# Attention with the high and low halves of v in one matmul of 66 columns, and x loaded already turned

## What is computed

```
q, k, v = (x @ W + b for W, b in ...)          # split in 12 heads of 32
scores  = q @ k.T / sqrt(32) + beta * adj
scores  = where(adj > 0, scores, -9e15)
out     = softmax(scores) @ v
```

## Time and profile before

| | |
|---|---|
| median of 3 runs | 2648.01 us (2646.37 to 2648.55) |
| the profiled execution | 2648.33 us |
| its span, first to last instruction | 2646.3 us |
| mean granted TensorE clock | 0.984 of full speed |
| busy: PE, PEld, DVE, ACT, POOL | 95%, 71%, 80%, 78%, 84% |
| HBM read, written | 35.92 MB, 12.58 MB |

### The profile page before, as it was taken

The page is one execution under the profiler, slowest core; times in us unless marked ns, Lnnn a source line. Parts: engine busy times, 40 slices in busy tenths (PEclk is TensorE's granted clock), DMA queues, the critical chain, the costliest instruction groups (busy, mean ns, idle before and its releaser), DMA issues.

```text
span 2646.3 us, 91774 instructions
## 1 busy us (share of the span) xinstructions
PE 2513.5 (95%) x33856; PEld 1892.1 (71%) x33856; DVE 2112.3 (80%) x8230; ACT 2075.7 (78%) x5844; POOL 2230.9 (84%) x3340
## 2 busy tenths in 40 slices
PE   5799999999999999999999999999999999999985
PEld 4667677777777777777777777777777777777753
DVE  6687787877778888888888888888888888888874
ACT  6667877778778888888888788788788888888765
POOL 5488888888888898898888888888888888888874
PEclk9899999999999999999999999999999999999997
DMA  6834545545445555545545555554545555554533
GB/s 176 176 68 83 97 85 97 96 83 97 89 87 97 95 90 97 97 89 95 97 89 100 93 90 98 96 91 93 96 95 92 93 99 88 96 97 88 94 55 71
DMA packets 846822, 251.63 MB, mean 95 GB/s; under 512 B 805552, under 2 KB 845616, under 8 KB 846384
## 3 DMA queue, kind: packets, MB, share of 16 engines
q1 hardware_dynamic: 837920, 230.83, 50.3%
q10 hardware_dynamic: 8464, 14.94, 1.9%
HBM read 35.92 MB, written 12.58 MB: 18 GB/s over the span
## 4 chain that ended last, share of the span: by engine, by line
POOL 35%; PE 23%; DVE 16%; ACT 13%; issue 7%; DMA 5%; SPq 1%; DVEq 0%; ACTq 0%; POOLq 0%
POOL region L750 6%; ACT region L870 5%; DMA region<-region 4%; POOL region L739 4%; DVE region L1138 4%; PE bank L966 3%; PE bank L957 3%; PE bank L968 3%; PE bank L967 3%; PE bank L959 3%; PE bank L958 3%; ACT region L876 3%; POOL ab L766 3%; POOL region L790 2%; DVE small L1144 2%
## 5 line engine op out<-in xcount | busy, mean ns | idle before, releaser
L957 PE MATMUL bank<-region,w_hi 128*128 128x128 f16 x3960 | 690.4, 220 | 35.6 <-DVE w_lo L1075 14.0
L959 PE MATMUL bank<-region,w_lo 128*128 128x128 f16 x3960 | 690.0, 220 | 0.0
L958 PE MATMUL bank<-region,w_hi 128*128 128x128 f16 x3960 | 690.0, 220 | 0.0
L966 PE MATMUL bank<-w_hi,region 128*128 128x384 f16 x1815 | 595.5, 328 | 10.4 <-DMA region<-region 9.2
L967 PE MATMUL bank<-w_lo,region 128*128 128x384 f16 x1815 | 594.3, 327 | 0.0
L968 PE MATMUL bank<-w_hi,region 128*128 128x384 f16 x1815 | 594.2, 327 | 0.0
L750 POOL TENSOR_TENSOR region<-region 128x512 f16<-128x512 f32 x330 | 382.9, 1161 | 117.7 <-ACT region L876 116.6
L870 ACT ACTIVATE region<-region,small 128x128 f32<-128x128 f32 x1320 | 419.2, 389 | 53.6 <-DVE small L1144 44.1
L957 PEld LDWEIGHTS bank<-region,w_hi 128*128 128x128 f16 x3960 | 389.4, 98 | 60.8 <-issue 36.2
L958 PEld LDWEIGHTS bank<-region,w_hi 128*128 128x128 f16 x3960 | 389.8, 98 | 14.8 <-issue 9.9
L959 PEld LDWEIGHTS bank<-region,w_lo 128*128 128x128 f16 x3960 | 389.9, 98 | 0.0
(11 more groups left out here) (246 smaller groups left out, 8238.0 us busy)
## 6 DMA issues: line engine op xcount, KB each, us to landing
region<-region SPq DMA_TRANSPOSE x825, 3.0
last_unit<-w_dram ACTq DMA_DIRECT2D x19, 576.0 KB, 6.2
x<-x_dram SPq DMA_DIRECT2D x55, 192.0 KB, 2.3
out_dram<-region SPq DMA_DIRECT2D x55, 192.0 KB, 2.2
adj<-adj_dram SPq DMA_DIRECT2D x55, 64.0 KB, 2.2
mask<-adj_t_dram SPq DMA_DIRECT2D x55, 64.0 KB, 2.4
rows<-rows_dram ACTq DMA_DIRECT2D x5, 576.0 KB, 4.4
last_unit<-last_unit SPq DMA_TRANSPOSE x135, 3.1
```

Of the source, the lines that this page charges most:

```text
L957: pe.matmul(dst, lhsT=w_hi[:, w, k, cols], rhs=t_hi[u][:, k, :], start=(k == 0), stop=False)
L958: pe.matmul(dst, lhsT=w_hi[:, w, k, cols], rhs=t_lo[u][:, k, :], start=False, stop=False)
L959: last = pe.matmul(dst, lhsT=w_lo[:, w, k, cols], rhs=t_hi[u][:, k, :], start=False, stop=(k == DT - 1))
L966: pe.matmul(dst, lhsT=t_hi[u][:, k, :], rhs=w_hi[:, w, k, :], start=(k == 0), stop=False)
```

## The change

Five things change.

1. In attend, v_hi and v_lo of a head stand side by side as one moving operand of 66 columns. Two matmuls a head instead of three: p_hi x (v_hi, v_lo) to 66 columns, then p_lo x v_hi added to the first 33. ScalarE copies the first 33 of each head out, and a new VectorE step adds the other 33 to the copy. This add now frees the bank.
2. The host passes x also turned. It is loaded first, into the place of z; ScalarE and GpSimd write the halves straight to t_hi and t_lo, and the first DMA transpose of a unit falls away. x and the adjacency are loaded after ScalarE's cast. The load into the slot waits for the norm (886) of unit i - 7, not for line 1256.
3. denominator moves from GpSimd to VectorE: two one-column operations at the end of delta_di, a reciprocal in the place of the power.
4. minus_adjacency moves from GpSimd to ScalarE.
5. All wish times of the plan and the tables SHIFTED and ARRIVES are new (PERIOD 22.1046 becomes 22.0705), so all engines' lists change order; the weight counters follow the list's own order (nth).

```diff
-    "attend": lambda s: {...}.get(s, (SCALAR, "attend", s))
+    "attend": lambda s: {...}.get(s, (VECTOR, "attend", s))
+        x_t = [a[:, 0:D].rearrange("p (t n) -> p t n", n=N) for a in z_at]
+        v_both = [a.bitcast(F16).rearrange("p (a h c) -> p a h c", a=2, c=HS) for a in v_at]
+        def two_parts(made):
+            return made[:, 0:2 * GO].rearrange("p (h a c) -> p h a c", a=2, c=HS)
...
 SyncE
-            def load(i, k):
+            def load_turned(i, k):
...
-                    sp.wait_ge(*mixed_out.at(i - UNITS, "added", 3))
+                    sp.wait_ge(*scalar_done.at(i - UNITS, "normed", 3))
+                sp.dma_start(x_t[i % UNITS], x_t_d[i]).then_inc(loaded.of(i), 16)
+            def load(i, k):
+                sp.wait_ge(*cast.at(i, "x", 0))
                 sp.dma_start(x[i % UNITS], x_d[i]).then_inc(loaded.of(i), 16)
                 sp.dma_start(adj[i % UNITS], adj_d[i]).then_inc(loaded.of(i), 16)
...
 GpSimd
+                if k == 0:
+                    pool.tensor_tensor(t_lo[u], x_t[u], t_hi[u], ALU.subtract).then_inc(low_made.of(i), 1)
+                    return
...
-            def minus_adjacency(i, k):
-                pool.wait_ge(*mixed_out.at(i, "delta_gcn", 1))
-                pool.tensor_scalar(minus_adj[u], adj[u], -1.0, None, ALU.mult).then_inc(gpsimd_done.of(i), 1)
-            def denominator(i, layer):
-                pool.wait_ge(*mixed_out.at(i, "delta_di", layer))
-                pool.tensor_scalar(col(u, DENOM), col(u, ZSUM), 1e-10, col(u, DSUM), ALU.mult, ALU.add).then_inc(gpsimd_done.of(i), 1)
-                pool.wait_ge(*gpsimd_done.at(i, "sum", layer))
-                pool.tensor_tensor(col(u, INVERSE), col(u, DENOM), constant(MINUS_ONE), ALU.pow).then_inc(gpsimd_done.of(i), 1)
...
 ScalarE
-                act.wait_ge(w_lo_made, n - STAGES + 1)
+                act.wait_ge(w_lo_made, nth(VECTOR, WEIGHT_ORDER[n - STAGES]))
...
-                    act.wait_ge(*loaded.at(i, "in"))
-                    src = x
+                    act.wait_ge(*loaded.at(i, "turned"))
+                    act.activation(t_hi[i % UNITS], x_t[i % UNITS], ACT.Copy).then_inc(cast.of(i), 1)
+                    return
...
-                act.activation(z_at[u][:, t * GO:(t + 1) * GO], bank("attend", s, i)[:, 0:GO], ACT.Copy).then_inc(scalar_done.of(i), 1)
+                act.activation(o_un[u][:, t * HG:(t + 1) * HG, :], two_parts(bank("attend", s, i))[:, :, 0, :], ACT.Copy).then_inc(scalar_done.of(i), 1)
...
+            def minus_adjacency(i, k):
+                act.wait_ge(*mixed_out.at(i, "delta_gcn", 1))
+                act.activation(minus_adj[u], adj[u], ACT.Copy, scale=-1.0).then_inc(scalar_done.of(i), 1)
...
 TensorE
-                        pe.wait_ge(*scalar_done.at(j, "o", n))
+                        pe.wait_ge(*numbers.at(j, "heads", n))
...
-                pe.wait_ge(*landed.at(i, "x", TURN_OF[w]))
+                if TURN_OF[w] == 0:
+                    pe.wait_ge(*low_made.at(i, "x", 0))
+                else:
+                    pe.wait_ge(*landed.at(i, "x", TURN_OF[w]))
...
-                    dst = bank("attend", s, i)[:, g * HS:(g + 1) * HS]
+                    dst = two_parts(bank("attend", s, i))[:, g, :, :]
-                    pe.matmul(dst, lhsT=pt_hi[u][:, g, :], rhs=v_hi[u][:, h, :], start=True, stop=False)
-                    pe.matmul(dst, lhsT=pt_hi[u][:, g, :], rhs=v_lo[u][:, h, :], start=False, stop=False)
-                    last = pe.matmul(dst, lhsT=pt_lo[u][:, g, :], rhs=v_hi[u][:, h, :], start=False, stop=True)
+                    pe.matmul(dst, lhsT=pt_hi[u][:, g, :], rhs=v_both[u][:, :, h, :], start=True, stop=False)
+                    last = pe.matmul(dst[:, 0, :], lhsT=pt_lo[u][:, g, :], rhs=v_hi[u][:, h, :], start=False, stop=True)
...
 VectorE
-                    dve.wait_ge(*gpsimd_done.at(i, "minus"))
+                    dve.wait_ge(*scalar_done.at(i, "minus"))
+            def attend(i, s):
+                u, t = i % UNITS, s % DT
+                heads = o_un[u][:, t * HG:(t + 1) * HG, :]
+                dve.wait_ge(*scalar_done.at(i, "o", s))
+                dve.tensor_tensor(heads, two_parts(bank("attend", s, i))[:, :, 1, :], heads, ALU.add).then_inc(numbers.of(i), 1)
...
-                                         op1=ALU.add, accum_out=col(u, DSUM)).then_inc(mixed_out.of(i), 1)
+                                         op1=ALU.add, accum_out=col(u, DSUM)).then_inc(numbers.of(i), 1)
+                dve.wait_ge(*numbers.at(i, "row sum", layer))
+                dve.tensor_scalar(col(u, DENOM), col(u, ZSUM), 1e-10, col(u, DSUM), ALU.mult, ALU.add).then_inc(numbers.of(i), 1)
+                dve.wait_ge(*numbers.at(i, "denominator", layer))
+                dve.reciprocal(col(u, INVERSE), col(u, DENOM)).then_inc(mixed_out.of(i), 1)
...
 host
+        "x_t_dram": _np.ascontiguousarray(a["x"].reshape(B, N, DT, 128).transpose(0, 3, 2, 1)),
```

More of the change, by code:

```diff
@@ new lines @@
+    (POOL, "turn", 1): (-615.369, 0.869, 1.111, ((SCALAR, "turn", 1),), ()),
+    (VECTOR, "delta_gcn", 1): (-610.860, 0.199, 0.407, ((SCALAR, "u_gcn", 1),), ()),
+    (VECTOR, "project", 7): (-605.018, 0.463, 0.741, ((SCALAR, "project", 7),), ()),
+    (SCALAR, "attend", 4): (-585.092, 0.170, 0.300, ((PE, "attend", 4),), ()),
+    (POOL, "bias", 8): (-585.084, 0.955, 1.090, ((SCALAR, "project", 8),), ()),
+    (POOL, "inner", 2): (-578.725, 0.780, 0.900, ((SCALAR, "inner_spread", 2),), ()),
+    (SCALAR, "norm", 2): (-560.881, 0.598, 0.740, ((POOL, "residual", 2),), ()),
@@ new lines @@
+    (SCALAR, "norm", 3): (-328.787, 0.597, 0.740, ((POOL, "residual", 3),), ()),
+    (SCALAR, "project", 6): (-328.735, 0.370, 0.570, ((PE, "project", 6),), ()),
+    (PE, "project", 17): (-321.463, 1.466, 1.660, ((SYNC, "turn", 5),), ()),
+    (SYNC, "turn", 2): (-314.258, 1.240, 3.600, ((VECTOR, "turn", 2),), ()),
+    (VECTOR, "u_di", 1): (-311.228, 0.364, 0.632, ((PE, "u_di", 1),), ()),
+    (VECTOR, "delta_low", 1): (-311.002, 0.480, 0.460, ((SCALAR, "delta", 1),), ()),
+    (VECTOR, "add_bias", 11): (-309.625, 0.460, 0.560, ((PE, "project", 11), (POOL, "low", 9)), ()),
@@ new lines @@
+    (SCALAR, "delta", 1): (-186.860, 0.190, 0.310, ((VECTOR, "delta_di", 1),), ()),
+    (VECTOR, "turn", 4): (-183.196, 0.442, 0.718, ((SCALAR, "turn", 4),), ()),
+    (POOL, "inner", 3): (-170.708, 0.780, 0.900, ((SCALAR, "inner_spread", 3),), ()),
+    (SCALAR, "norm", 0): (-170.159, 0.599, 0.740, ((POOL, "residual", 0),), ()),
+    (PE, "scores", 0): (-166.086, 0.360, 0.610, ((VECTOR, "project", 2), (POOL, "low", 0), (POOL, "low", 1)), ()),
+    (PE, "project", 1): (-165.576, 1.513, 1.710, ((POOL, "turn", 0),), ()),
@@ new lines @@
+    (SCALAR, "project", 8): (-76.615, 0.370, 0.570, ((PE, "project", 8),), ()),
+    (VECTOR, "attend", 1): (-76.478, 0.200, 0.320, ((SCALAR, "attend", 1),), ()),
+    (POOL, "low", 9): (-73.290, 0.880, 1.120, ((SCALAR, "project", 9),), ()),
+    (VECTOR, "u_di", 0): (-72.133, 0.385, 0.656, ((PE, "u_di", 0),), ()),
+    (PE, "u_di", 1): (-70.812, 0.512, 0.720, ((SYNC, "turn", 4),), ()),
+    (VECTOR, "residual", 1): (-70.774, 0.480, 0.620, ((VECTOR, "gain", 1),), ()),
+    (SCALAR, "attend", 5): (-70.263, 0.170, 0.300, ((PE, "attend", 5),), ()),
@@ new lines @@
+    (POOL, "scores", 1): (177.943, 1.150, 1.420, ((SCALAR, "scores", 1),), ()),
+    (POOL, "bias_x", 0): (193.093, 0.961, 1.245, ((SYNC, "load", 0),), ()),
+    (POOL, "bias", 5): (254.100, 0.955, 1.090, ((SCALAR, "project", 5),), ()),
+    (VECTOR, "add_bias", 1): (257.477, 0.460, 0.720, ((PE, "project", 1),), ((SYNC, "store", 0),)),
+    (SCALAR, "minus_adj", 0): (442.166, 0.190, 0.300, ((VECTOR, "delta_gcn", 1),), ()),
+    (SCALAR, "turn", 5): (453.393, 0.413, 0.600, ((SCALAR, "norm", 2),), ()),
@@ L600, in graph_layers @@
         scalar_done = signal("scalar_done", SCALAR, {"attend": ("o",), "u_gcn": ("e_gcn",),
[L601 removed]
+                                                     "u_di": ("e_di",), "norm": ("normed",), "minus_adj": ("minus",), "delta": ("high delta",),
                                                      "spread": ("minus mean", "spread"),
@@ L621, in graph_layers @@
         gpsimd_done = signal("gpsimd_done", POOL, lambda name, k: {
-            "turn_delta": ("triangles",), "sides": ("upper", "lower"), "minus_adj": ("minus",),
-            "sums": ("sum", "row scale"),
+            "turn_delta": ("triangles",), "sides": ("upper", "lower"),
             "inner": ("inner root",) if k < 2 else ("variance", "inner root"),
@@ L663, in low_of, with nth @@
             return v_lo[u][:, :, 0:HD]
+        def nth(engine, w):
+            return 1 + [k for name, k, _ in sequence(engine) if name == "weight"].index(w)
         def load_weight(eng, n):
@@ L814, in _ @@
             for name, k, i in sequence(POOL):
```

(2 more changed lines are left out.)

417 lines of the change are left out of this document (194 added, 223 removed), and 60 rows, old and new, of the table SHIFTED.

## The result

The changed kernel takes 2656.3 us (median of 5 runs, 2652.22 to 2658.13) beside 2648.0 us (5 runs, 2642.6 to 2648.55) before: a ratio of 1.0033, 95% interval 1.0019 to 1.0046. It is 0.3% slower; the forecast was 2616.5 us, faster, with a range up to 2642. The profiled execution took 2656.3 us, of which 2653.8 us is span.

What follows compares the result with a forecast made beforehand. The prediction took PE to bound the middle. From 2648.3 us it subtracted 33.8 for matmuls, added 5 for VectorE, subtracted 3 for the start, the rest 0: 2616.5 us, range 2598 to 2642.

Steps and rivals of the forecast that it cites:

- What bounds the kernel: Middle, 800 to 2400 us: PE, busy 1578 of 1600 us, bounds; what it sheds comes off unless another engine takes over.
- Term 1: Attend's matmuls on PE: a step falls from 0.31 us to 222 ns, over 384 steps 33.8 us less.
- The weight loads: Attend on PE: four loads a step fall away; they run beside the matmuls, so costed at nothing.
- Rival D: Attend's weight loads were in line: 96 ns for each of 1536 removed, 147 us less, 2501 us; chance 0.01.
- Term 2: VectorE's new adds and denominator: busy 90% of the middle, 5 us more for PE's waits, bounds 0 and 30.
- Term 3: GpSimd sheds 2.2 us a unit, ScalarE gains one pass of 0.27 us; effect on the time 0.
- Term 4: One DMA transpose of x fewer a unit, the next unit's load into the slot later: about cancel, 0.
- Term 5: Start: PE begins at about 9.2 us, 4.8 us sooner; 3 us of gain taken, bounds 0 and 6.
- Term 6: End: the last units run in another order; 0, plus or minus 10 us.
- B: Attend's banks, freed too late by VectorE's add, stop PE at line 1169: slower, 2680 us; chance 0.09.
- A: VectorE at 90% delays scores and exponentials, PE under 97% of the middle: 20 us back, about 2632; chance 0.16.
- C: Attend's wide matmul costs as much as two, a step stays at 0.31 us: 2650 us, within 0.2%; chance 0.06.

Runs made afterwards that it cites:

- b_pe8: The kernel before with one of the three matmuls of each head in attend left out (39.6 us less PE work): 2633.27 us, ratio 0.9953.
- k_noadd: The kernel before, own lists kept, with the wide matmul alone and no VectorE adds, low half left out of the result: 2632.62 us, ratio 0.9951.
- a_pe12: The changed kernel with its 66-column matmul split into two of 33, twelve matmuls a step again: 2658.27 us, ratio 1.0056 to the kernel before.
- k_relief: The kernel before, own lists kept, with only GpSimd's denominator moved to VectorE and minus_adjacency to ScalarE: 2651.28 us, ratio 1.0017.
- k_banks: The kernel before with the attend part alone, adds included, in its own lists, PSUM banks dealt anew for the later release: 2672.53 us, ratio 1.011.
- s_tail: The changed kernel with new shifts searched for units 50 to 63 alone: 2651.96 us, ratio 1.0013 to the kernel before.
- a_thin: The changed kernel with VectorE's new adds cut to one column a head: 2646.84 us, ratio 1.0009 to the kernel before.
- s_before: The kernel before, same operations, with wish times, shifts and period searched anew: 2637.65 us, ratio 0.9954.

## Why the prediction was wrong, point by point

**What bounds the kernel: wrong, and this is the step that failed.** "The middle is bound by PE, and what PE sheds there comes off the span." PE's busy share and its short waits were read right, but they show that PE has little slack in the present order, not that the order closes up when PE gets faster. Shedding 39.6 us gave 12.6 (b_pe8), shedding 27 gave 12 (k_noadd), adding 27 cost 6 (a_pe12). In the middle itself 0.62 us a unit less gave 0.12 and 0.42 us less gave about 0.1 at most; before 800 us most of it came off. So the step holds there and fails for the middle, of which it was said. The short waits of the kernel before, 0.4 us at most for the turn step, can be read as the sign of a second bound close behind: b_pe8 made them longer, 17.3 us in 28 waits where they were 7.2 in 27.

```profile
PE bank L957 <- DVE region L1116: 17.3, 28, 0.7
```

That this second bound is a loop through other engines is argued, not shown by a run that isolates it. The chain of waits of the kernel before pointed to other engines too, and I didn't read it in the middle. There it runs through GpSimd from 1212 to 1229 us, while PE is busy beside it:

```profile
1207.81 1.29 ACT region L870 x4
1209.12 0.63 ACT region L876
...
1212.07 1.16 POOL region L750
...
1219.61 1.12 POOL region L790
...
1228.75 0.57 POOL small L803
...
1230.08 0.18 DVE small L1237
```

Nor is GpSimd the one bound: k_relief took 2.2 us a unit from it, onto VectorE and ScalarE, and the middle stayed at 16150 / 529 = 30.53 units.

**Term 1, the matmuls:** right in kind, too large in size. The step takes 0.23 to 0.24 us, not 0.222: the wide matmul takes the 30 ns of the estimate, but a 33-column one between wide ones takes 27 ns (the median) and not 25.8. The work saved is some 27 us, within the bounds. Its price in time, the 33.8 us of the sum, should have been about 12 by k_noadd.

**The weight loads** cost nothing in line, as the trace said: four fewer a step came with 0.07 us less, not 0.4. Rival D is out, and with it the reading of the Trainium skill's figure (TensorE: Matmul & The Clock Gate, LDWEIGHTS) as time in line; this case's trace disagrees with that reading.

**Term 2, the adds:** the duration was right, 284 ns where I said 0.29 us. VectorE's load was over-estimated (84% of the middle, not 90), in part because its mask step became shorter. The price was wrong for lists that weren't made for the adds. In the lists of the kernel before the adds cost 41 us, above the bound of 30 that I set. In the changed kernel, whose lists are made for them, cutting their duration by 129 ns is worth 6.4 us; what the whole instruction costs there wasn't tried. I bounded it by PE's waits at the bank that the add frees. k_banks removed those waits and the cost stayed, so they don't measure it. That it is the six more places a unit where VectorE's list stands between other engines is my reading; a shortage of banks altogether isn't ruled out.

**Term 3, GpSimd and ScalarE:** the forecast of 0 holds; k_relief gives +0.17%. **Term 4** can't be judged by itself: in old lists the late region costs 2.8%, and how far the new lists absorb it wasn't tried. **Term 5, the start:** PE starts at 8.53 us where I said 9.2, but by 100 us no head start is left: 884 / 505 = 1.75 units are done after and 966 / 529 = 1.83 before. PE stood still for 12.2 us at one of the first attends, for the DMA transpose of p, where its longest such wait was 8.4 us in the kernel before:

```profile
58.85 0.24 PE L1029 MATMUL bank<-v,region 128*128 128x66 f16 x1 [12.20 <-DMA region<-region]
```

By 800 us the changed kernel is 0.18 of a unit ahead, 7 us. The earlier start and PE's lighter work share this, and no run parts them.

**Term 6, the order at the end:** put at 0, plus or minus 10, with the reason that nothing told which. It is where the changed kernel falls behind the kernel before: level or ahead at 2000 us, 7.5 us longer at the end, with 15 us lost from 2000 to 2400 us and partly regained behind. s_tail took back about 5 with other shifts.

**The sum.** Taking the runs of this study as prices, -12 for the matmuls, nothing for the start and 5 for the end leave 15 us to explain between 2641 and 2656. The stretches of the traces say where they are. Against k_noadd, which has the lighter matmuls and nothing else, the changed kernel's span is 21.5 us longer. By 800 us it is 0.15 of a unit or 6 us behind, in the middle it loses 3 us (30.47 units against 30.55), and behind 2000 us some 12. So in its own lists the adds, the late region z and the rest cost little in the middle, and the end costs most. How the adds, region z and the lists share these costs isn't settled, since each can be measured only in lists made for something else. **The rivals.** B had the right sign and the wrong place: no wait on line 1169 stands high in the changed kernel, the lists had avoided it and bought it off with the wait on line 1285. A has its sign, PE under 97% of the middle, but a size of 20 us where 40 were missing, and its engine is shown only in part: thinner adds gave back 6.4 us (a_thin). C is out: the wide matmul is cheap. Not among the rivals was the case that came, in which all the savings are real and only a part of them is on the path.

## What to carry to other kernels

An engine that is busy for 98% isn't thereby the bound: in a program of fixed lists its relief pays only as far as nothing else is close behind, and b_pe8 got back 5 us of 19 in such a stretch, so first leave the work out (one run, like b_pe8) and take that gain as the ceiling. When work moves to an engine that has room by its busy share, don't take its price as nothing: 111 us of adds on a VectorE that was busy for 80% cost 41 us in lists not made for them, and 25 us still when each add was cut to 160 ns. A change of 0.3% can't be told from what the order of the lists does by chance unless both versions are also timed in other orders; reordering the kernel before gained 0.46%, about what the lighter matmuls alone won (0.49%, k_noadd).

## What the runs showed of the hardware

A 33-column matmul costs 25.8 ns from start to start among its like the earlier trace rows. When it alternates with 66-column ones, in the changed kernel from 800 to 2400 us, the next start comes 30 ns behind a wide one and 27 ns behind a narrow one (medians of 968 and 763 pairs). A second width in a step shouldn't be priced from a run of one width. The strided operand (two pieces of 33 columns) showed no cost of its own: 30 ns, where the line through 128 and 384 columns gives 29.7. One pass on VectorE was not constant in duration: the mask step, 128 x 128 between tiles in on-chip memory, took 955 ns on average from 800 to 2400 us in the kernel before (the first row) and 395 ns in s_before (the second), which differ in order alone. Over the whole kernel its median is 986 and 352 ns. What stands beside it on GpSimd differs too, and the cause wasn't tried:

```profile
L1111 DVE SCALAR_TENSOR_TENSOR mask<-adj,minus_beta,mask 128x128 f32<-128x128 f32 x36 | 34.4, 955 | 1.3
```

```profile
L1111 DVE SCALAR_TENSOR_TENSOR mask<-adj,minus_beta,mask 128x128 f32<-128x128 f32 x35 | 13.8, 395 | 1.2
```
